# A chunk's output sum is read from PSUM by VectorE instead of ScalarE, behind the chunk's third product

## The reference

```python
def _block(x, dc_w, dc_b, of_w, of_b, dw, db):
    h = jax.nn.relu(_deconv2d(x, dc_w, dc_b))
    offset = _conv2d(h, of_w, of_b, PAD)
    return jax.nn.relu(_deform_conv2d(h, offset, dw, db))
...
in_cur = x + in_prev
x = _block(in_cur, ...)          # four blocks
...
x_cat = jnp.concatenate((x, in_module), axis=1)
offset = _conv2d(x_cat, fin_off_w, fin_off_b, PAD)
return _deform_conv2d(x_cat, offset, fin_dcn_w, fin_dcn_b)
```

## Time and profile before

| | us |
|---|---|
| median of 3 runs | 4393.4 (4388.14 to 4399.32) |
| the profiled execution | 4396.28 |
| its span, first to last instruction | 4394.4 |
| mean granted TensorE clock | 0.934 of full speed |

### The profile page before, as it was taken

The page is one execution under the profiler, slowest core; times in us unless marked ns, Lnnn a source line. Parts: engine busy times, 40 slices in busy tenths (PEclk is TensorE's granted clock), DMA queues, the critical chain, the costliest instruction groups (busy, mean ns, idle before and its releaser), DMA issues.

```text
span 4394.4 us, 221688 instructions
## 1 busy us (share of the span) xinstructions
PE 3849.4 (88%) x81888; PEld 2958.5 (67%) x81888; DVE 2931.0 (67%) x5838; ACT 2782.9 (63%) x6651; POOL 1145.0 (26%) x655
## 2 busy tenths in 40 slices
PE   4998799599879869968986996998699999699998
PEld 3676577477657657756765774676577777477776
DVE  4785687388568648846865884785577774477775
ACT  2886588288468738837864882885355554255554
POOL 0341243034134314403422440331121110112111
PEclk8999899799979979988997997999799999799999
DMA  3442544344254334424424442543666664566664
GB/s 118 123 128 68 133 125 113 82 121 127 63 134 126 97 92 126 128 69 128 126 79 110 127 118 73 133 126 113 165 150 155 155 148 127 130 149 152 154 154 108
DMA packets 244839, 533.52 MB, mean 121 GB/s; under 512 B 61200, under 2 KB 151824, under 8 KB 227216
## 3 DMA queue, kind: packets, MB, share of 16 engines
q1 hardware_dynamic: 194224, 498.67, 44.3%
q10 hardware_dynamic: 50240, 29.89, 2.3%
HBM read 471.87 MB, written 56.45 MB: 120 GB/s over the span
## 4 chain that ended last, share of the span: by engine, by line
PE 61%; SPq 21%; issue 7%; DMA 3%; POOLq 3%; ACT 2%; DVE 2%; POOL 0%; ACTq 0%; DVEq 0%; PEld 0%; PEldq 0%
PE P L542 22%; PE PS L560 22%; SPq L388 10%; SPq L380 10%; PE P L513 7%; PE PS L573 7%; POOLq L256 2%; ACT H L840 1%; PE PS L513 1%; DMA X<-x_dram 1%; DMA HB<-off_store 1%; PE P L528 1%; DVE FOFF L1024 1%; DMA off_store<-FOFF 0%; DVE ST L1028 0%
## 5 line engine op out<-in xcount | busy, mean ns | idle before, releaser
L909 DVE TENSOR_TENSOR A<-P,YC 121x384 f32<-121x384 f32 (+1 forms) x4608 | 2312.0, 549 | 959.0 <-ACT YC L760 762.2
L542 PE MATMUL P<-HL,SEL 32*121 32x384 f16 (+1 forms) x21504 | 1730.0, 303 | 323.1 <-issue 216.2
L760 ACT ACTIVATE YC<-P 121x384 f32<-121x384 f32 (+1 forms) x4608 | 1732.5, 445 | 109.5 <-PE P L542 70.8
L542 PEld LDWEIGHTS P<-HL,SEL 32*121 32x121 f16 (+1 forms) x21504 | 1124.0, 116 | 697.1 <-issue 351.6
L560 PE MATMUL PS<-A,VT 121*32 121x80 f32 (+1 forms) x40960 | 1336.5, 249 | 64.2 <-DMA VT<-ht_store 31.7
L560 PEld LDWEIGHTS PS<-A,VT 121*32 121x32 f32 (+1 forms) x40960 | 1087.6, 116 | 366.1 <-issue 203.7
L737 ACT ACTIVATE SMP<-PS 128x480 f32<-128x480 f32 (+3 forms) x1152 | 593.0, 515 | 636.5 <-PE PS L560 630.4
L1089 POOL CAST HL<-DIST 128x1152 f16<-128x1152 f32 x320 | 365.9, 1143 | 2217.2 <-DVE DIST L914 2217.2
L1091 POOL TENSOR_TENSOR HL<-DIST,HL 128x1152 f16<-128x1152 f32 x320 | 769.5, 2405 | 131.6 <-issue 75.7
L727 ACT ACTIVATE DIST<-HB,CONST 128x1152 f32<-128x1152 f32 x320 | 400.8, 1253 | 307.9 <-DMA HB<-off_store 192.8
L573 PE MATMUL PS<-SMP,CW 128*64 128x128 f32 x7424 | 475.9, 277 | 5.4 <-ACT SMP L737 5.4
(11 more groups left out here) (56 smaller groups left out, 740.8 us busy)
## 6 DMA issues: line engine op xcount, KB each, us to landing
HB<-off_store SPq DMA_DIRECT2D x2560, 72.0 KB
VT<-ht_store SPq DMA_DIRECT2D x256, 512.0 KB
VT<-ht_store SPq DMA_DIRECT2D x768, 132.0 KB
VT<-ht_store SPq DMA_DIRECT2D x256, 88.0 KB
off_store<-FOFF SPq DMA_DIRECT2D x160, 128.0 KB, 2.6
H<-x_dram SPq DMA_DIRECT2D x5, 2048.0 KB, 14.2
ht_store<-A ACTq DMA_DIRECT2D x32, 256.0 KB, 3.3
ht_store<-VT ACTq DMA_DIRECT2D x32, 256.0 KB, 4.0
```

The costliest lines, as they stand in the source:

```text
L542: mm = nc.tensor.matmul(dst, SEL[q, table, 0:sh.npos], hats, start=part == 0, stop=part == 1)
L760: nc.scalar.activation(YC[0:sh.npos, g % X_SLOTS, 0:sh.size], P[0:sh.npos, g % Y_SLOTS, 0:sh.size], ACT.Copy).then_inc(y_ready, 1)
L909: return nc.vector.tensor_tensor(dst, x, y, ALU.mult)
```

## The change

`read_sum` leaves ACT and becomes a function of DVE. It waits for the same two semaphores, does one `tensor_scalar` (add the bias; maximum with 0 except in the final layer) from PS into TMP, and counts up `ps_free`. In the loop it stands behind product 2 (`g == sh.sum_after + 1`); the residual stays behind product 3. At the end of a step it stands just ahead of each `add_residual`.

```diff
-                def read_sum(c, half):
-                    wait_alone(act, ps_full, (c + 1) * sh.ps_uses + 2)
-
-                    wait_alone(act, res_done, c + 1)
-                    out_act(layer, PS[:, :], half, final).then_inc(ps_free, 1)
...
-                            if b == sh.batches - 1 and g == sh.sum_after and before >= sh.lag:
-                                read_sum(c - sh.lag, (half + sh.lag) % 2)
...
-                    if sh.lag == 2:
-                        read_sum(CHUNKS - 2, 0)
...
-                    read_sum(CHUNKS - 1, 1)
...
+                def read_sum(c, half):
+
+                    wait_alone(dve, ps_full, (c + 1) * sh.ps_uses + 2)
+
+                    wait_alone(dve, res_done, c + 1)
+                    tmp = TMP[:, half, :].rearrange("p (y w x) -> p y w x", y=BLK, w=BLOCKS)
+                    sums = PS[:, 0:CPX].rearrange("p (w y x) -> p y w x", w=BLOCKS, y=BLK)
+                    if final:
+                        ready = nc.vector.tensor_scalar(tmp, sums, bias_of(layer, 1), None, ALU.add)
+                    else:
+                        ready = nc.vector.tensor_scalar(tmp, sums, bias_of(layer, 1), 0.0, ALU.add, ALU.max)
+                    ready.then_inc(ps_free, 1)
...
+                            if before >= sh.lag and b == sh.batches - 1 and g == sh.sum_after + 1:
+                                read_sum(c - sh.lag, (half + sh.lag) % 2)
...
                     if sh.lag == 2:
+                        read_sum(CHUNKS - 2, 0)
                         add_residual(CHUNKS - 2, BANDS - 1, 0)
+                    read_sum(CHUNKS - 1, 1)
                     add_residual(CHUNKS - 1, BANDS - 1, 1)
```

## The result

| | before | after |
|---|---|---|
| median, us | 4393.5 (4 runs) | 4907.9 (4899.3 to 4931.2, 4 runs) |
| ratio | | 1.118, interval 1.114 to 1.122 |
| the profiled execution | 4396.3 | 4901.2 |
| mean granted TensorE clock | 0.934 | 0.891 |

The account below looks back on a forecast made before the run. It took the path to run mostly through PE, whose sample part 0 would wait for DVE's read. 4396.3 + 254 (blocks' steps) - 18 (late transfers) + 50 (final steps) = 4682; forecast 4680 us, range 4605 to 4760.

Parts of the forecast that it names:

- What bounds the kernel: Whole kernel: the path runs mostly through PE, busy for 88% of the span and carrying 61% of the last chain.
- ACT's gain of nothing: Blocks' steps: YC 2 to 4 come 0.25 us earlier without the read on ACT, but nobody takes that; counted at nothing.
- The read, 0.345 us: DVE's new read of the sum from PSUM takes 0.345 us, with ends at 0.28 and 0.62.
- Rival (1): POOL's cast holds DVE's new read until about 205.27 instead of 204.52: 180 us on top, 4860 us; chance 7%.
- PE's wait in a block's step, 1.38 us: Sample part 0 waits for DVE's read behind product 2 and starts at 204.57 instead of 203.19, a 1.38 us stall.
- What comes back, 0.30: Blocks' steps: after a late part 0, PE waits less for its spreads, regaining 0.30 us an iteration; bounds 0 and 0.5.
- 5.3 to 5.5 given as a sign: Sign in the new profile: from part 0 to the next distance it is 5.3 to 5.5 us.
- Late transfers: Longer iterations let SP's late window queue catch up: 4.5 of some 6 us go in each of four steps, -18 us.
- The final steps, 50 us: In the final steps PE's part 0 starts 0.80 us late, 62 times, and nothing comes back: +50 us.
- the gain of product 2: Final steps: with YC 2 copied earlier, DVE starts product 2 at 3509.35 instead of 3509.62; without it, 1.05 us late.
- The sum without the clock: The terms added without any fall of PE's clock: 4682 us for the profiled execution, 4680 us forecast, 6.5% slower.
- Rival (2): PE idles in each iteration, so its clock falls: 0.5 us for each of two parts, 240 us more, 4920 us; chance 4%.

Follow-up runs that it names:

- hats_again: The changed kernel, with PE repeating the two x hats matmuls of spread 1 twice more in the blocks' steps, ahead of the sum: 4700.5 us, ratio 1.069.
- sums_again: The changed kernel, with PE computing the first three taps of the sum twice in the blocks' steps: 4715.7 us, ratio 1.074.
- warm: The changed kernel, with PE repeating the two x hats matmuls of spread 4 four more times in the blocks' steps: 4793.9 us, ratio 1.091.
- clamp_behind: The changed kernel, with DVE's clamp moved behind the read in the blocks' steps: 4602.2 us, ratio 1.049.
- act_late: The kernel before, ACT still reading the sum, but behind YC 4 and with an added wait for product 2: 5042.9 us, ratio 1.149.

## Why the prediction was right and wrong

- **What bounds the kernel, and ACT's gain of nothing**: right. No run shows a gain from the work that leaves ACT.
- **The read, 0.345 us**: right, 0.343 on average of 256 (L925) and of 64 (L923). Rival (1), that POOL's cast holds it, is out: the read at 207.81 lies under the cast of 207.60 to 208.74 and takes 0.34. The Trainium skill's rule that ScalarE is closer to PSUM and VectorE closer to SBUF ("Advanced Engine Details and Errata", "The Read-Write Bubble") did not show in the durations: 0.34 here against ACT's 0.37.
- **PE's wait in a block's step, 1.38 us**: right. Part 0 starts 4.22 us behind the distance (203.99 to 208.21) instead of 2.85 (200.34 to 203.19), which is 1.37 later; 1.30 of it shows as idle time, released by the read.
- **What comes back, 0.30**: right. From part 0 at 208.21 to the distance at 213.77 are 5.56 us, against 5.85 before: 0.29, though 5.56 is just outside the 5.3 to 5.5 given as a sign. Iterations of hats_again, at full clock, average 9.66, which is 1.08 more than 8.58.
- **Late transfers**: right. Steps 1 and 2 are nearly equal now, 326.2 and 327.7 us from the first sum to the last, against 263.6 and 268.7. As the clock falls in both, hats_again is the better witness: 296.2 and 296.3, and 296.9 in step 4. So 5 and 6 us went, where 4.5 had been let go.
- **The final steps, 50 us**: 60 measured. The mis-sized term is the gain of product 2. Part 0 starts 1.64 us behind the start of its spreads (3901.11 to 3902.75), before it was 0.70 (3508.72 to 3509.42): 0.94 late, not 0.80. I had let product 2 start 0.27 earlier with YC 2. In fact it waits for its x hats (1.42 <-PE P L542) and gains only 0.13.
- **The sum without the clock**: 4680 forecast for the median, 4700 measured with hats_again. Of these 20 us, 10 are the final steps.
- **The clock**: here it failed. The sum puts the fall of the clock at nothing; it cost 207 us. Rival (2) named it and put the time at 4920 (4908 measured), but got 4%, and the range stopped at 4760. The step that failed is the sentence "that wait was longer than the 1.38 us here, and only that one row bears on it". That is an argument from a lack of rows, and it cuts both ways: no row of before showed PE pausing 1.3 us in every iteration at full clock. The range should have reached the rival's price.

  The trace of before held more than that one row, and I had not laid it beside the rival. In step 2 PE waited 1.48 us for windows, longer than the 1.38, and the granted clock around it was 1.00 (the part first, then the stretch); in step 6, at 2020.66, 1.34 us, with 1.00 again from 2010 to 2030.

```profile
515.41 1.04 PE L560 MATMUL PS<-A,VT 121*32 121x80 f32 x48 [1.48 <-DMA VT<-ht_store]
```
```profile
505.00:520.00 15.00, 13.38 (x322) 9.79 (x322) 11.91 (x25) 11.72 (x27) 7.11 (x4) 1.00 0.44 117
```

  A single pause of that size left the clock alone there; in the changed kernel one comes in each iteration, and no row of before could tell what that does.

  That 240 and 207 lie so close is partly luck. The rival has 0.5 us for each of two parts in every iteration. The runs show 1.4 to 3.1 us in something over half of them (15 of 27 between 130 and 400 us) and nothing in the others. In the iteration that starts at 213.77 it is one part, 1.83 instead of 1.04, and the spreads behind it, 1.56 instead of 0.89; the next part takes 1.04 again. And the guess that went with the rival, that the pause itself is what counts, is refuted by sums_again, hats_again and warm.

## What to carry to other kernels

When a read that frees a PSUM bank moves to another engine, look at what stands ahead of it in that engine's order, and compare the moment of release with the moment at which TensorE asks; here the duration and the engine of the read hardly mattered. If a change makes TensorE pause in each iteration of a loop that ran at full clock, the fall of the clock is a term to be priced, and the range has to reach it, until a row with such a pause in each iteration shows it away. Here it cost 0.86 us an iteration beside a pause of 1.30, and nothing beside one of 0.63 (clamp_behind). And a moved instruction that reads two SBUF operands on VectorE is to be laid beside GpSimd's rows first.

## What the runs showed of the hardware

The residual on DVE (two inputs from SBUF) waits for the POOL instruction under which it begins and ends 0.14 to 0.16 us after it: 201.05 to 202.12 with a cast ending at 201.98 (1.07 us), 202.24 to 204.04 with a subtraction ending at 203.89 (1.80 us), 206.59 to 209.15 with one ending at 208.99 (2.56 us). Without POOL it takes 0.34. In the changed kernel it begins so late under the cast that this hardly shows: 208.53 to 208.88, the cast ending at 208.74. And in act_late one that began at 217.43, 0.04 before the cast's end, took 0.35, though POOL's subtraction began at 217.65 while it still ran. So the held ones began well before POOL's instruction ended (0.46 us in the earlier trace rows, more in the three above). The read from PSUM and the products, under the same casts, kept 0.34 and 0.55 us. The Trainium skill, "SBUF — State Buffer", section "Who interferes with whom", says that a DVE instruction with two SBUF inputs contends with a GpSimd instruction that reads SBUF; these rows agree with it.

The granted clock fell to 0.97 in a stretch in which PE was busy for 249.96 of 250 us, and held at 1.00 in one with 216 of 250 and a pause of 1.31 us in each iteration. With eight added matmuls at one place it held where they ran over 128 rows (1.51 us) and fell where they ran over 32 rows (1.3 us).
